# Value product of an attention kernel on high and low parts, with the transposed probabilities handled in another order

## The reference, cut to what matters

```python
q = (lat @ Wq)...; k = (kv_in @ Wk)...; v = (kv_in @ Wv)...
sim = jnp.einsum('bhqd,bhfd->bhqf', q, k)
sim = jnp.where(full_mask[:, None, None, :] == 0, -jnp.inf, sim)
alphas = jax.nn.softmax(sim, axis=-1)
out = jnp.einsum('bhqf,bhfv->bhqv', alphas, v)
x = x + out @ Wo
...
h = silu(einsum('td,edh->teh', xt, w1)) * einsum('td,edh->teh', xt, w3)
y = einsum('teh,ehd->ted', h, w2)          # 8 experts, top 2, and a shared one
```

## Time and profile before

| | |
|---|---|
| three runs, us | 1152.14, 1158.64, 1159.47 (median 1158.64) |
| profiled execution, us | 1153.85, with a span of 1152.1 |
| granted TensorE clock, mean | 0.989 of full speed |
| busy: PE, DVE, ACT, POOL | 1083.4, 926.4, 792.1, 615.2 us |
| DMA engines busy, mean | about half of the span |

### The profile page before, as it was taken

How to read it: one execution, slowest core, us unless ns; L and a number is a source line. 1 busy time by engine, 2 the same in 40 slices (tenths; PEclk the granted TensorE clock), 3 DMA queues, 4 the chain that set the end, 5 groups by cost and what they waited for, 6 DMA issues and landing times.

```text
span 1152.1 us, 28179 instructions
## 1 busy us (share of the span) xinstructions
PE 1083.4 (94%) x7720; PEld 941.8 (82%) x7720; DVE 926.4 (80%) x4095; ACT 792.1 (69%) x2924; POOL 615.2 (53%) x717
## 2 busy tenths in 40 slices
PE   6899999999999999999999999999999999999976
PEld 6788887888888788888888888888888888888755
DVE  3878887888887788888888888778888788888756
ACT  4887777776777677777776677776777776777631
POOL 5555555555555455555555555555555555554421
PEclk9999999999999999999999999999999999999979
DMA  5455455555455555455555555555455555545531
GB/s 153 141 165 155 152 169 161 163 153 154 150 170 155 162 147 159 145 172 161 171 155 154 154 158 170 168 152 149 137 168 168 168 151 154 155 149 163 157 117 33
DMA packets 248717, 176.81 MB, mean 153 GB/s; under 512 B 29424, under 2 KB 215408, under 8 KB 248560
## 3 DMA queue, kind: packets, MB, share of 16 engines
q1 hardware_dynamic: 247376, 173.96, 50.8%
q10 hardware_dynamic: 1184, 1.05, 0.3%
HBM read 103.35 MB, written 71.56 MB: 152 GB/s over the span
## 4 chain that ended last, share of the span: by engine, by line
SPq 26%; PE 24%; DVE 21%; DMA 11%; issue 11%; ACT 5%; POOL 0%; DVEq 0%; POOLq 0%; ACTq 0%
SPq L335 13%; DMA pT<-probsT_dram 9%; SPq L363 6%; PE bank L860 5%; PE bank L873 4%; PE bank L815 4%; PE bank L817 3%; PE bank L816 3%; SPq L328 3%; DVE logits L671 3%; DVE probsT L686 3%; ACT probs L557 3%; SPq L369 3%; DVE h L704 2%; DVE g_eq L603 2%
## 5 line engine op out<-in xcount | busy, mean ns | idle before, releaser
L453 POOL TENSOR_TENSOR probs<-probs,rdenom 128x512 f32<-128x512 f32 x256 | 266.4, 1041 | 405.0 <-DVE rdenom L680 400.4
L557 ACT ACTIVATE probs<-logits,neg_max 128x128 f32<-128x128 f32 x1024 | 398.7, 396 | 0.9 <-DVE neg_max L671 0.9
L873 PEld LDWEIGHTS bank<-kvT,tT 128*128 128x128 f32 x2048 | 268.8, 192 | 120.3 <-issue 106.8
L860 PE MATMUL bank<-pT,kv_f 128*128 128x512 f32 x512 | 269.3, 607 | 44.2 <-DMA pT<-probsT_dram 43.9
L873 PE MATMUL bank<-kvT,tT 128*128 128x128 f32 x2048 | 270.7, 275 | 0.0
L716 DVE TENSOR_TENSOR cT_lo<-bank,cT_hi 128x512 fp32r<-128x512 f32 x256 | 175.2, 685 | 83.8 <-ACT cT_hi L527 83.7
L671 DVE CUSTOM_DVE_ANT_0 logits<-bank,mask_add 128x128 f32<-128x128 f32 x1024 | 232.6, 282 | 6.1 <-PE bank L873 5.9
L527 ACT CAST cT_hi<-bank 128x512 fp32r<-128x512 f32 x256 | 150.0, 586 | 113.1 <-PE bank L860 112.5
L557 ACT ACTIVATION_READ_ACCUMULATOR probs<-logits,neg_max 128x1 f32 x1024 | 197.6, 193 | 0.0
L512 ACT ACTIVATE h_tanh<-bank 128x256 f32<-128x256 f32 x160 | 61.6, 385 | 180.7 <-PE bank L817 178.3
L686 DVE STREAM_TRANSPOSE probsT<-probs 128x512 f32<-128x512 f32 x256 | 176.0, 688 | 0.7 <-issue 0.5
(11 more groups left out here) (102 smaller groups left out, 1996.4 us busy)
## 6 DMA issues: line engine op xcount, KB each, us to landing
probsT_dram<-probsT SPq DMA_DIRECT2D x256, 256.0 KB, 2.4
pT<-probsT_dram SPq DMA_DIRECT2D x1024, 64.0 KB, 2.2
gates<-gates_dram SPq DMA_DIRECT2D x62, 256.0 KB, 4.2
kv_raw<-in_ctx SPq DMA_DIRECT2D x32, 128.0 KB, 2.8
kv_raw<-in_x SPq DMA_DIRECT2D x32, 128.0 KB, 2.9
mask_raw<-in_mask_BxS_ik SPq DMA_DIRECT2D x32, 128.0 KB, 3.4
x_res<-in_x SPq DMA_DIRECT2D x32, 128.0 KB, 2.7
out<-out_sb SPq DMA_DIRECT2D x32, 128.0 KB, 3.0
```

Of the source, the lines that this page charges most:

```text
L453: nc.gpsimd.tensor_tensor(by_pair, by_pair, rdenom[n][:, :].unsqueeze(2).unsqueeze(3).broadcast_to([P, PAIRS, P // QUAD, QUAD]), ALU.mult) ...
L557: nc.scalar.activation(probs[c % 4][:, :, r, :], logits[c % 2][:, r, :].rearrange("p (c k) -> p c k", k=QUAD), ACT.Exp, bias=neg_max[c % 2 ...
L860: nc.tensor.matmul(C_ps[c % 2][:, :], kv_f[g % 3][:, kl % 4, :], pT[c % 3][:, :], start=True, stop=True).then_inc(C_in_psum, 1)
L873: last = nc.tensor.matmul(S_ps[c % 2][:, P * r:P * (r + 1)], tT[:, kl % 4, hd:hd + 2, :], kvT[g % 2][:, kl % 4, :], start=True, stop=True)
```

## The change

The probabilities' way back and the value product change.

- The value product takes high and low parts: `kv_hi`, `kv_lo` from GpSimd (key steps 7 and 8, at k=1 of the next frame), `pT_hi` from ScalarE, `pT_lo` from VectorE for even halves and from GpSimd for odd ones. Both parts of half e-3 are made in half e, and TensorE uses them in half e+1.
- VectorE transposes the probabilities of half e (not e-1), as nearly the last thing of half e.
- SP, in half e, first issues the other DMAs, then loads half e-1, then stores half e. The load now waits for the low part that last read its `pT` buffer. Gates go to DRAM at k=5 and 6 and come back at k=0, kv is loaded at k=7, out is stored at k=3, x_res at k=2.
- `kv_f` has one buffer and `kv_hi`, `kv_lo` three, the context table `cT` one in place of two. Its first half (kl=0 to 3) is written again once the projection has read it (`W_front_done`).

```diff
 def load_probs(s):                                      # SP
     sp.wait_ge(probsT_stored[n], 16 * (s // 3 + 1))
-    after(sp, C_in_psum, s - 2)
+    if s >= 3:
+        sp.wait_ge(pT_lo_ready[(s - 3) % 2], (s - 3) // 2 + 1)
...
-    if has_half(e - 1):
-        store_probs(e - 1)
-    if has_half(e - 2):
-        load_probs(e - 2)
+    if k == 0 and has(j, p, 3, NG + 1):                  # gates back from DRAM
...
+    if k in (5, 6) and has(j, p, 2, NG):                 # gates to DRAM, two DMAs in each
...
+    if k == 7 and has(j, p, -2, NG - 4):
+        load_kv(j, p + 3)
+    if has_half(e - 1):
+        load_probs(e - 1)
+    if has_half(e - 0):
+        store_probs(e - 0)

 # GpSimd, key steps
+    nc.gpsimd.tensor_copy(kv_hi[g % 3][:, :, :], kv_f[:, :, :])
+    nc.gpsimd.tensor_tensor(kv_lo[g % 3][:, :, :], kv_f[:, :, :], kv_hi[g % 3][:, :, :].bitcast(fp32),
+                            ALU.subtract)
 # GpSimd, after centring
+    if has_half(e - 3) and (e - 3) % 2 == 1:
+        pool.wait_ge(pT_hi_ready, c + 1)
+        after(pool, C_in_psum, c - 1)
+        nc.gpsimd.tensor_tensor(pT_lo[1][:, :], pT[c % 3][:, :], pT_hi[1][:, :].bitcast(fp32), ALU.subtract)

 # ScalarE, before the high part of C
+    if has_half(e - 3):
+        act.wait_ge(pT_loaded[c % 3], 64 * (c // 3 + 1))
+        after(act, C_in_psum, c - 1)
+        nc.scalar.copy(pT_hi[c % 2][:, :], pT[c % 3][:, :])

 # VectorE
-    if has_half(e - 1):                                  # after the reciprocal
-        nc.vector.transpose(probsT[c % 2][:, :], probs[c % 4]...)
...
+    if has_half(e - 3) and (e - 3) % 2 == 0:             # before the low part of C
+        dve.wait_ge(pT_hi_ready, c + 1)
+        nc.vector.tensor_tensor(pT_lo[0][:, :], pT[c % 3][:, :], pT_hi[0][:, :].bitcast(fp32), ALU.subtract)
...
+    if has_half(e):                                      # after the low part of C
+        dve.wait_ge(probs_ready, c + 1)
+        nc.vector.transpose(probsT[c % 2][:, :], probs[c % 4]...)

 # TensorE
-    pe.wait_ge(pT_loaded[c % 3], 64 * (c // 3 + 1))
+    pe.wait_ge(pT_lo_ready[c % 2], c // 2 + 1)
...
-    nc.tensor.matmul(C_ps[c % 2][:, :], kv_f[g % 3][:, kl % 4, :], pT[c % 3][:, :], start=True, stop=True)
+    matmul3(C_ps[c % 2][:, :], kv_hi[g % 3][:, kl % 4, :], kv_lo[g % 3][:, kl % 4, :],
+            pT_hi[c % 2][:, :], pT_lo[c % 2][:, :])
```

More of the change, by code:

```diff
@@ L62, in xattn_moe_ffn_kernel @@
         kv_n = sb("kv_n", [P, GB, D])
-        kv_f = [sb(f"kv_f{n}", [P, GB, D]) for n in range(3)]
+        kv_f = sb("kv_f", [P, GB, D])
+        kv_hi = [sb(f"kv_hi{n}", [P, GB, D], f32r) for n in range(3)]
+        kv_lo = [sb(f"kv_lo{n}", [P, GB, D], f32r) for n in range(3)]
         kvT = [sb(f"kvT{n}", [P, GB, P]) for n in range(2)]
@@ L78, in xattn_moe_ffn_kernel @@
         pT = [sb(f"pT{n}", [P, PAIRS * P]) for n in range(3)]
+        pT_hi = [sb(f"pT_hi{n}", [P, PAIRS * P], f32r) for n in range(2)]
+        pT_lo = [sb(f"pT_lo{n}", [P, PAIRS * P], f32r) for n in range(2)]
         attnT = sb("attnT", [P, GT])
@@ L107, in xattn_moe_ffn_kernel @@
         h_silu = sb("h_silu", [P, GT])
-        h = [sb(f"h{n}", [P, NT + 1, GT]) for n in range(2)]
         out_sb = [sb(f"out_sb{n}", [P, TT, D]) for n in range(2)]
@@ L342, in frame @@
                     e = HALVES * i + k
-                    if has_half(e - 1):
-                        store_probs(e - 1)
-                    if has_half(e - 2):
-                        load_probs(e - 2)
-                    if k == 0 and has(j, p, -1, NG - 3):
-                        load_kv(j, p + 2)
+                    if k == 0 and has(j, p, 3, NG + 1):
+                        sp.wait_ge(gates_stored, 64 * (i - 2))
+                        after(sp, h_routed_done, NT * (i - 3))
+                        for a in range(2):
+                            sp.dma_start(gates[FH * a:FH * (a + 1), :, :],
+                                         gates_dram.rearrange("(r a) t -> a r t", a=2)[a, :, :].partition_broadcast(FH)
+                                         ).then_inc(gates_loaded, 16)
+                    if k == 1 and has(j, p, -1, NG - 3):
                         load_mask(j, p + 2)
-                    if k == 0 and has(j, p, 4, NG + 2):
-                        store_out(i - 1)
-                    if k == 1 and has(j, p, 0, NG - 1):
+                    if k == 2 and has(j, p, 0, NG - 1):
                         after(sp, x1_step, 3 * (i - 2) + 1)
@@ L357, in frame @@
                                      ).then_inc(x_res_loaded[p], 16)
-                    if k == 5 and has(j, p, 2, NG):
+                    if k == 3 and has(j, p, 4, NG + 2):
+                        store_out(i - 1)
+                    if k in (5, 6) and has(j, p, 2, NG):
                         sp.wait_ge(gate_step, GATE_STEPS * (i - 1))
                         after(sp, gates_loaded, 32 * (i - 2))
-                        for a in range(P // QUAD):
+                        for a in (0, 1) if k == 5 else (2, 3):
                             sp.dma_start(gates_dram.rearrange("e (t a q) -> e t a q", t=TT, a=P // QUAD)[:, :, a, :],
                                          g_denseT[QUAD * a:QUAD * a + E, :, :]).then_inc(gates_stored, 16)
[L365 to L371, removed]
+                    if k == 7 and has(j, p, -2, NG - 4):
[4 more added lines that the diff above has]
+                        store_probs(e - 0)
                 if i == NG + 2:
```

70 lines of the change are left out of this document (48 added, 22 removed).

## The result

The changed kernel takes 1276.1 us (median of 4 runs, 1274.87 to 1279.95), the kernel before 1157.64 beside it (4 runs, 1152.14 to 1159.47): a ratio of 1.1038 [1.0993, 1.1083]. The forecast of 1176 had the sign, but the time lies far outside its range of 1108 to 1203. The profiled execution took 1275.57 us, at a mean granted clock of 0.972 (before: 0.989). An estimate of what the clock can be worth: a mean of 0.972 is 71 us of the span at the lower of its two levels (1.2 in place of 2.4 GHz), one of 0.989 is 25 us. In the 46 us more TensorE loses at most half, so 23 of the 118 us.

The account below looks back on a forecast made before the run. The prediction took VectorE to bound part of each frame, DMA and TensorE the rest; VectorE's new halves summed to 35.05 us against 34.4, +21 us over 31 frames on 1153.85, giving 1176 us, range 1108 to 1203.

Parts of the forecast that it names:

- TensorE alone would need 31.4 us: TensorE per frame: 34.4 less 1.6 from the cheaper product and 1.4 of vanished probability waits.
- GpSimd is free for it, but not at any moment: GpSimd's low parts and key steps: about 6 us a frame more, 615 to some 810 us busy; timing carries the price.
- holding: VectorE operations reading two SBUF operands wait for GpSimd; at k=3, 4, 5 and 7 costed at 0.45, 0.35, 0.4, 0.6 us.
- Rival 3: Low parts at k=3, 4 wait 1.04 us, gate product 0.25 late: 1222 us, or 1199 for half; chance 0.15.
- I cost SP at nothing: SP's new load and store order adds nothing, and the 1.4 us a frame wait for probabilities goes.
- ScalarE: its bounds are 0 and 2 us a frame; I take 0: ScalarE's eight casts, 4.7 us a frame, hide under VectorE unless half of them delay the exponentials.
- a gain of 0.2 us a half: TensorE's value product: three rounded products at 0.66 us replace a float32 one of 0.86; 1.6 us a frame.
- The sum itself: VectorE's eight new halves add to 35.05 us against an average frame of 34.4: +0.67, over 31 frames +21 us.
- VectorE's halves: VectorE times forecast for k=0 to 7: 3.25, 4.3, 5.6, 6.25, 4.0, 3.9, 2.9, 4.85 us.
- its wait gone: VectorE's half k=6 falls from 3.70 to 2.9 us because its waiting disappears.
- The signs named in advance: Profile signs of a right forecast: DMA wait gone, transposes waiting for normalisation, low part 0.6 to 1.6 us, products 0.22 apiece.
- VectorE over 88% busy: Sign of a right forecast: VectorE's busy share rises above 88%, from 80% before.

Follow-up runs that it names:

- spread_only: Kernel before with only SP's other DMAs spread over the halves, ahead of store e-1 and load e-2; 1108.63 us, ratio 0.9588.
- order_store_first: Kernel before with DMAs spread, transpose of the same half late, store e ahead of load e-1, float32 product kept; 1135.56 us, ratio 0.9831.
- order_sf_casts: order_store_first plus ScalarE's cast of every half of the probabilities into a buffer nobody reads; 1171.83 us, ratio 1.0127.
- short_both_sf: Changed kernel with store ahead of load and both probability low parts cut to 4 of 512 columns; 1187.97 us, ratio 1.029.
- store_first: Changed kernel with SP's store of half e ahead of the load of half e-1, nothing else; 1275.88 us, ratio 1.1037.
- order_alone: Kernel before with only the new order on SP and VectorE, load ahead of store, float32 product kept; 1207.54 us, ratio 1.0467.
- short_gp_low: Changed kernel with GpSimd's probability low part alone cut to 4 of 512 columns; 1245.12 us, ratio 1.0785.
- gp_low_first: Changed kernel with GpSimd's low part right behind the normalisation, ahead of gating and centring; 1259.72 us, ratio 1.092.

## Why the prediction was wrong

From before to changed in steps that were each run. Each price holds for this order of the steps alone, since bounds hide one another:

| step | us | difference |
|---|---|---|
| before | 1156 | |
| other DMAs of SP spread (spread_only) | 1109 | -47 |
| transpose of the own half, late; load e-1 behind store e (order_store_first) | 1136 | +27 |
| ScalarE's casts (order_sf_casts) | 1172 | +36 |
| three products, key steps, links with low parts of 4 columns (short_both_sf) | 1188 | +16 |
| low parts of 512 columns (store_first) | 1276 | +88 |
| load ahead of store (changed) | 1276 | 0, but +72 without the split |

- **"TensorE alone would need 31.4 us", and so less than VectorE: the step that failed.** The forecast took the sum of VectorE's halves for the time and TensorE's waits for nothing. But TensorE was the bound. In spread_only it is idle for 35 us in all and a frame takes 33.05 us; in the changed kernel it is idle for 187 us, 160.6 of them ahead of product C for the low parts, 5.0 us a frame. From the one to the other the span grew by 163 us and TensorE's idle time by 152. What the runs showed in place of a time set by VectorE is TensorE's work plus this wait; the sum has the wait only inside VectorE's k=1, not as idle time of the engine that fills the frame.
- **"GpSimd is free for it, but not at any moment": the right place, the wrong price.** It was looked for at VectorE (holding), and GpSimd's low part was sized by the normalisation: 1.04, measured 1.28. When it would be ready was not far off, 1.35 us into VectorE's k=1, and 1.51 in the frame above, whose k=1 begins at 627.97. What was not counted is that TensorE stands idle up to then: 3.44 us median at k=1 against 1.0 before. Rival 3 named the place, TensorE late at k=1, with 0.25 us.
- **"I cost SP at nothing": failed.** The issues were counted and fit. That the load now asks for the store directly ahead of it in the same queue was not worked out: 2.2 us of landing, four issues and a store in a circle, 4.3 us a half. In order_alone it gives 1207 us; in the changed kernel it is hidden. The wait for pT by DMA did go, and spread_only shows why: it was where SP's other DMAs stood.
- **"ScalarE: its bounds are 0 and 2 us a frame; I take 0": failed**, and it lies inside its own bounds: 36/31 = 1.2 us a frame, in the kernel without the split. Free time on the engine did not cover casts that stand ahead of cT_hi in an in-order queue.
- **TensorE, a gain of 0.2 us a half: nearly right for the product (0.17 where it starts without a wait), wrong for the kernel (0.09),** since in six of eight halves the first of the three takes 0.1 us longer, mostly behind a wait or a late weight load.
- **The sum itself.** It compares 35.05 us with the average frame of 34.4, but its halves are changes to the frame that was read, whose eight halves add up to 33.9. Like with like it would be +1.1 us a frame and 1188 us, still 88 us short.
- **VectorE's halves: right where only VectorE and GpSimd's holding decide** (0, 3, 4, 5). At k=6 "its wait gone" and at k=7 4.85 were wrong, by 1.0 and 1.3 us, most of the 2.8 us by which the sum missed the frame. The waits there were taken for the DMA's and TensorE's lateness. In spread_only, where TensorE hardly waits, these halves take 3.72 and 6.05 us all the same: VectorE waits there for results of TensorE at TensorE's own pace. The changed kernel's VectorE timeline at k=6 and 7 (in brackets, the idle time and its releaser):

```profile
617.35 0.69 DVE L749 TENSOR_TENSOR cT_lo<-bank,cT_hi 128x512 fp32r<-128x512 f32 x1 [0.61 <-ACT cT_hi L559]
...
620.36 0.42 DVE L716 TENSOR_TENSOR out_sb<-bank,x 128x256 f32<-128x256 f32 x1 [0.78 <-PE bank L861]
620.70 1.78 DVE L739 TENSOR_TENSOR pT_lo<-pT,pT_hi 128x512 fp32r<-128x512 f32 x1
```

- **The signs named in advance:** the transpose's wait for the normalisation came (26.0 us) and the wait by DMA went. VectorE's low part of 0.66 to 1.78 us came too, and the products, with 0.23 us apiece, nearly. VectorE over 88% busy and TensorE waiting at the gate product did not come: VectorE is at 82%, so it was never the only bound, and the sum of its halves could not be the time.

Not settled: how the 88 us of the low parts divide between GpSimd's queue (31 us by short_gp_low alone), VectorE's work and their meeting; which share of the 27 us is the transpose's and which the load's; which share of the 36 us is the casts' waiting and which their work; and how much of each difference between the split versions is the clock's, at most 23 us between the changed kernel and the one before.

## What to carry to other kernels

Read the chain before the busy shares: a queue that only issues DMAs was 26% of it, and spreading those DMAs gained 47 us, where the whole change, of which it is a part, lost 118. Ask which engine's work fills the frame once the waits are gone, here TensorE's (33.05 us), and count what the change makes that engine wait for. When work is handed to an idle engine, write down everything that stands ahead of it in that engine's queue at that moment, and who waits for its end; the free share says nothing of it. Where a queue both stores and loads back the same data, keep a half's distance between the store and the load that asks for it.

## What the runs showed of the hardware

- A store to DRAM and the load that waits for it in one queue: 2.24 us from the store's issue to the first load's (order_alone). In the same rows a store takes SP 0.38 us to issue, four loads 1.75 to 1.93.
- In the rounded type a product of 512 columns takes 0.23 to 0.24 us from start to start (changed kernel, k=6), the first one 0.34 after TensorE had waited; the float32 product 0.86 in two records.
- After 2.02 us of waiting, gp_low_first's products stood 0.43 us apart at a granted clock of 0.50, in place of 0.23.
- GpSimd takes 1.28 us for a 128x512 subtraction with rounded output, 1.04 for a float32 multiplication of that shape.
- The holding doesn't go by the size of the operation that is held: a VectorE operation of 4 columns took 1.25 us (short_both_sf), and GpSimd is held in its turn by VectorE's (the normalisation that begins at 629.43 in the changed kernel, behind a VectorE low part that began at 628.89, took 1.49 us in place of 1.04). The Trainium skill (SBUF — State Buffer, Who interferes with whom) states the exclusion as a lock, in which the order of issue decides who waits; both rows agree.
